# A decoder layer on one core: reordering the background work of cross-attention, and the maxima rows' way into the operand stack

## The reference

```python
# _L0_xattn_ref(target, source, ...): 16 heads of 16, 512 positions t (targets) and s (sources)
q = Wq @ layernorm(x)  + bq        # [256, 512]
k = Wk @ ctx + bk
v = Wv @ ctx + bv
# per head: scores = q^T k / sqrt(16), masked; softmax over s; out = probabilities @ v
# x2 = x + out, then the feed-forward
```

## Time and profile before

| | us |
|---|---|
| median of 3 runs | 2346.96 (2342.14 to 2351.12) |
| profiled execution | 2347.5, its span 2345.7 |
| TensorE busy | 2167.7 (92%) |
| VectorE busy | 1597.0 (68%) |
| ScalarE, GpSimd busy | 797.7, 761.3 |
| main loop of the cross-attention | 1500.2 to 2047.3 of the span |

### The profile page before, as it was taken

How to read it: one execution, slowest core, us unless ns; L and a number is a source line. 1 busy time by engine, 2 the same in 40 slices (tenths; PEclk the granted TensorE clock), 3 DMA queues, 4 the chain that set the end, 5 groups by cost and what they waited for, 6 DMA issues and landing times. The chain is left out here.

```text
span 2345.7 us, 35412 instructions
## 1 busy us (share of the span) xinstructions
PE 2167.7 (92%) x11638; PEld 1524.1 (65%) x11638; DVE 1597.0 (68%) x2871; ACT 797.7 (34%) x1845; POOL 761.3 (32%) x533
## 2 busy tenths in 40 slices
PE   6899999999999999999999997599888899879998
PEld 4677777778787777778778785233333333267776
DVE  6658888788786558788788774477777778542221
ACT  1323323322323323323323322155555546642221
POOL 3235334434444334434434433211122221212121
PEclk9999999999999999999999998798989978989999
DMA  5211011011102201011101006634555434311110
GB/s 197 87 40 52 16 49 51 24 40 51 46 19 99 82 20 52 24 41 51 43 22 51 32 4 118 114 64 81 93 107 90 87 74 84 99 60 54 54 36 19
DMA packets 58981, 142.27 MB, mean 61 GB/s; under 512 B 9118, under 2 KB 23910, under 8 KB 53894
## 3 DMA queue, kind: packets, MB, share of 16 engines
q1 hardware_dynamic: 57142, 138.98, 23.4%
q10 hardware_dynamic: 1744, 2.08, 0.3%
HBM read 89.93 MB, written 17.55 MB: 46 GB/s over the span
## 5 line engine op out<-in xcount | busy, mean ns | idle before, releaser
L1614 DVE TENSOR_REDUCE x_mx<-x_pm 128x1 f32<-128x512 f32 x512 | 316.5, 680 | 58.2 <-PE x_pm L1706 55.8
L1472 ACT ACTIVATE x_E<-x_pd 128x512 f32<-128x512 f32 x512 | 264.8, 604 | 214.1 <-PE x_pd L1720 213.4
L1083 PE MATMUL a_pj<-q_big,a_wqk_h 128*128 128x512 f32 x1024 | 290.1, 405 | 1.4 <-POOL a_wqk_l L628 1.4
L1099 PE MATMUL a_pj<-a_wvg_h,q_big 128*128 128x512 f32 x1024 | 286.0, 406 | 1.1 <-DVE a_rm L787 1.0
L1099 PEld LDWEIGHTS a_pj<-a_wvg_h,q_big 128*128 128x128 f32 x1024 | 185.4, 188 | 51.8 <-DVE a_rm L787 2.4
L787 DVE TENSOR_TENSOR a_rm<-a_pj,a_rope 128x1024 f32<-128x1024 f32 x128 | 155.7, 1218 | 79.9 <-PE a_pj L1083 78.5
L1083 PEld LDWEIGHTS a_pj<-q_big,a_wqk_h 128*128 128x128 f32 x1024 | 182.9, 188 | 40.8 <-POOL a_wqk_l L628 1.9
L520 ACT ACTIVATE a_v<-a_pj 128x256 f32<-128x256 f32 x128 | 49.1, 384 | 415.6 <-PE a_pj L1099 415.6
L660 POOL TENSOR_TENSOR a_ogl<-a_ogf,a_ogh 128x512 fp32r<-128x512 f32 x64 | 81.7, 1298 | 285.4 <-ACT a_ogf L556 285.4
L1734 PE MATMUL x_pa<-x_E,x_vx 128*32 128x512 f32 x1024 | 152.2, 670 | 0.0
L859 DVE TENSOR_TENSOR a_acc<-a_po,a_acc 128x512 f32<-128x512 f32 x128 | 85.9, 687 | 92.7 <-PE a_po L1212 92.7
(11 more groups left out here) (219 smaller groups left out, 4624.9 us busy)
## 6 DMA issues: line engine op xcount, KB each, us to landing
a_qk_raw<-in_wqk SPq DMA_DIRECT2D x16, 1024.0 KB, 5.5
a_vg_raw<-in_wvg SPq DMA_DIRECT2D x16, 1024.0 KB, 4.9
a_wo_raw<-in_wo SPq DMA_DIRECT2D x16, 512.0 KB, 3.7
x_Q<-x_hi SPq DMA_DIRECT2D x20, 256.0 KB
x_K<-x_hi SPq DMA_DIRECT2D x20, 256.0 KB
a_acc<-in_w SPq DMA_DIRECT2D x6, 704.0 KB, 4.4
a_wt<-in_w SPq DMA_DIRECT2D x24, 176.0 KB, 2.3
weights_scratch<-a_wt SPq DMA_DIRECT2D x24, 176.0 KB, 1.9
```

The costliest lines, as they stand in the source:

```text
L1083: last = mm(pj[:, j % 2, :], wa[:, c, j * P:(j + 1) * P], xa[:, c, p * UT:(p + 1) * UT], start=k == 0, stop=k == 11)
L1099: last = mm(pj[:, tt % 2, :], xa[:, c, t0:t0 + P], wa[:, c, :], start=k == 0, stop=k == 11)
L1472: nc.scalar.activation(E[:, n % ESLOTS, :], pd[:, n % 3, :], ACT.Exp, scale=XD ** -0.5).then_inc(exp_done, 1)
L1614: nc.vector.reduce_max(mx[:, u % 2, at:at + 1], pm[:, k % 3, :], AX_X).then_inc(pm_done, 1)
```

## The change

- Projections of batch b + 2 move from G5 to G10 to G7 to G12, in the order key, query, value; takes, high halves and low halves with them (ScalarE's high halves to G8 to G11).
- The row statistics go to G5 and G6, both norms to G8, the inversions of the sums to G7 to G12 (in the last two batches one a step from G2 and from G10).
- On GpSimd the second `divide_and_add` goes between the key and the query low halves.
- SyncE: new FILLS and LATE; the load of x at G2 and not at G13 of the batch before; the stores at G3 and G15.
- The maxima rows go from mT straight to Q. VectorE's `max_rows` now waits for the landing of the previous quad's row.
- wv, the identity and the bf16 identity are loaded once, in stage one, and stay in SBUF. TensorE waits for the cross-attention's other constants two value projections later.
- At the end of stage one the low halves of the last output are subtracted by VectorE from PSUM; ogf isn't written there.

```diff
+        def order(b):
+            return (2, 3, 0, 1, 4, 5) if b > 1 else (0, 1, 2, 3, 4, 5)
         def projected(b, j):
-            return 6 * b + j - 4
+            return 6 * b + order(b).index(j) - 4
+        def halved(b, w):
+            return 4 * (b - 1) + order(b).index(2 * w + 1) + 1
+        def inverses(b, G):
+            if b + 2 < B:
+                due = {7: (-1, (0, 1)), 8: (-1, (2,)), 9: (-1, (3,)), 10: (0, (0,)), 11: (0, (1, 2)), 12: (0, (3,))}
+            else:
+                due = {**{2 + i: (-1, (i,)) for i in range(4)}, **{10 + i: (0, (i,)) for i in range(4)}}
+            n, parts = due.get(G, (0, ()))
+            return 2 * b + n, (parts if 2 * b + n >= 0 else ())
...
-        FILLS = {8: ((0, 0),), 10: ((0, 1), (0, 2)), 11: ((0, 3), (0, 4)), 14: ((0, 5), (1, 0)), 15: ((1, 1), (1, 4))}
-        LATE = {0: ((1, 5),), 2: ((1, 2), (1, 3))}
+        FILLS = {10: ((1, 0), (1, 1)), 11: ((1, 4), (1, 5)), 12: ((0, 0), (0, 1)), 13: ((0, 2),), 14: ((0, 3), (1, 2)), 15: ((1, 3), (0, 4))}
+        LATE = {0: ((0, 5),)}
...
             def rows(u):
                 sp.wait_ge(pm_done, turned_slot(u) + 1)
                 after(sp, row_in[u % 2], 32 * (u // 2))
-                sp.dma_start(max_dram[u % 2], mT[:].bitcast(F32)).then_inc(max_out, 16)
-                sp.wait_ge(max_out, 16 * u + 16)
                 for e in range(2):
                     sp.dma_start(Q[b % 3][64 * e + 53:64 * e + 54, 2 * g:2 * g + 2].rearrange("p h t -> p (h t)").bitcast(F32),
-                                 max_dram[u % 2, 8 * e:8 * e + 8, :].rearrange("(o a) t -> o (a t)", o=1)).then_inc(row_in[u % 2], 16)
+                                 mT[8 * e:8 * e + 8].bitcast(F32)).then_inc(row_in[u % 2], 16)
...
-                    if q == 3 and t >= 4 and t % 2 == 0:
-                        store(t // 2 - 2)
+                    if b and G in (3, 15):
+                        store(2 * b - 2 + (G == 15))
                     if b + 2 < B:
+                        if G == 2 and b:
+                            load_x(b + 2)
...
-                        if G == 13 and b + 3 < B:
-                            load_x(b + 3)
...
             def max_rows(u):
-                after(dve, max_out, 16 * u)
+                if u:
+                    dve.wait_ge(row_in[(u - 1) % 2], 32 * ((u - 1) // 2 + 1))
...
-                    if q >= 2 and t >= 2 and t % 2 == 0:
-                        invert(t // 2 - 1, q - 2)
-                    if q < 2 and t >= 3 and t % 2 == 1:
-                        invert((t - 3) // 2, q + 2)
                     G = 4 * (t % 4) + q
+                    n, parts = inverses(b, G)
+                    for i in parts:
+                        invert(n, i)
                     if b + 2 < B:
-                        if G < 2:
-                            norm_stats(b + 2, G)
-                        if 3 <= G < 5:
-                            norm(b + 2, G - 3)
-                        if 5 <= G < 11:
-                            take_projection(b + 2, G - 5)
+                        if 5 <= G < 7:
+                            norm_stats(b + 2, G - 5)
+                        if G == 8:
+                            norm(b + 2, 0)
+                            norm(b + 2, 1)
+                        if 7 <= G < 13:
+                            take_projection(b + 2, order(2)[G - 7])
...
             quad_scores(0, 1)
-            pe.wait_ge(const_in, N_CONST)
             project(0, 4)
             quad_scores(0, 2)
             project(0, 5)
             quad_scores(0, 3)
+            pe.wait_ge(const_in, N_CONST)
             project(1, 0)
...
+            def low_last(l):
+                for h in range(2):
+                    dve.wait_ge(ogh_done, 2 * l + h + 1)
+                    nc.vector.tensor_tensor(ogl[:, h, :], po[:, h, :], ogh[:, h, :].bitcast(F32), ALU.subtract).then_inc(ogl_done, 1)
```

More of the change, by code:

```diff
@@ L554, in high_out @@
                     nc.scalar.activation(ogh[:, h, :], po[:, h, :], ACT.Copy).then_inc(ogh_done, 1)
-                    after(act, ogl_done, 2 * l)
-                    nc.scalar.activation(ogf[:, h, :], po[:, h, :], ACT.Copy).then_inc(ogf_done, 1)
+                    if not final(l):
+                        after(act, ogl_done, 2 * l)
+                        nc.scalar.activation(ogf[:, h, :], po[:, h, :], ACT.Copy).then_inc(ogf_done, 1)
             def unit(n, g, p, k0):
@@ L1003, in core @@
                 gated(m, pm)
+                low_last(m)
                 normalised(5)
@@ L1492, in _ @@
                     G = 4 * (t % 4) + q
-                    if 6 <= G < 10 and t // 4 + 2 < B:
-                        high(t // 4 + 2, G - 6)
+                    if 8 <= G < 12 and t // 4 + 2 < B:
+                        high(t // 4 + 2, order(2)[G - 8])
             take_weighted(QUADS - 1)
@@ L1552, in _ @@
                     rsqrt(b + 2)
-                    for j in range(4):
-                        low(b + 2, j)
+                    low(b + 2, 2)
+                    low(b + 2, 3)
+                if b:
+                    divide_and_add(2 * b - 1)
+                if b + 2 < B:
+                    low(b + 2, 0)
+                    low(b + 2, 1)
                     values(b + 2, 0)
                     values(b + 2, 1)
-                if b:
-                    divide_and_add(2 * b - 1)
             divide_and_add(2 * B - 2)
@@ L1597, in take_projection @@
                         dve.wait_ge(x_in[1], 32)
-                    elif j == 0:
+                    elif b > 1 and j == order(b)[0]:
                         dve.wait_ge(stack_in[(b - 1) % 3], stacked(b - 1))
@@ L1766, in _ @@
                     G = 4 * (t % 4) + q
-                    if 5 <= G < 11 and b + 2 < B:
-                        project(b + 2, G - 5)
+                    if 7 <= G < 13 and b + 2 < B:
+                        project(b + 2, order(2)[G - 7])
                     if t + q:
@@ L1771, in _, with feed_forward @@
             weighted(QUADS - 1, 3)
-def feed_forward(nc, signals, spent, x2_in, raw, big, ident_in, identb_in, out):
+def feed_forward(nc, signals, spent, x2_in, raw, big, ident, identb, out):
     G = N_TOK // 512
@@ L2112, in decoder @@
                        x1.rearrange("(h b) t p d -> h p (b t) d", h=HALVES), a["w"], scalers, rebuilt, weights,
-                       big, xs, a["ctx"], a["mask"], a["wq"], a["wk"], a["bqk"], rows)
+                       big, xs, ident, identb, wv_t, a["ctx"], a["mask"], a["wq"], a["wk"], a["wv"], a["bqk"], a["identb"], rows)
         with Scope(nc, "x") as passing:
@@ L2117, in decoder @@
         w_raw = kept.sb("raw", [P, 3, NFLAT], BF16)
-        cross_attention(nc, of_cross, of_self.used, x1, a["ctx"], a["mask"], a["maskc"], a["wq"], a["wk"], a["wv"], a["bqk"], a["bv"],
-                        a["ident"], rows, maxima, x2, third, bv_t, w_raw, weights, big, xs)
+        cross_attention(nc, of_cross, of_self.used, x1, a["ctx"], a["mask"], a["maskc"], a["wq"], a["wk"], wv_t, a["bqk"], a["bv"],
+                        ident, rows, x2, third, bv_t, w_raw, weights, big, xs)
         of_self.close()
         of_ffn = kept.enter_context(Scope(nc, "sf"))
-        feed_forward(nc, of_ffn, of_cross.used, x2.rearrange("(g b) t p d -> g (b t) p d", b=2), w_raw, big, a["ident"], a["identb"],
+        feed_forward(nc, of_ffn, of_cross.used, x2.rearrange("(g b) t p d -> g (b t) p d", b=2), w_raw, big, ident, identb,
                      out.rearrange("(g b) (t p) d -> g (b t) p d", b=2, p=P))
```

49 lines of the change are left out of this document (21 added, 28 removed).

## The result

| | us |
|---|---|
| changed kernel | 2329.4 median of 20 runs (2306.14 to 2350.48) |
| kernel before, same chips | 2352.26 median of 20 runs (2342.14 to 2371.45) |
| ratio | 0.9876, 95% interval 0.9852 to 0.9899 |
| profiled execution | 2321.17, span 2319.4 (before 2345.7) |

What follows compares the result with a forecast made beforehand. It took VectorE's waits for late loads and sums, which stop TensorE and lower its clock in the cross-attention, as the bound. Terms -51.9, -6.0, -5.8, -3.0, -1.4, -1.6 sum to -69.7: 2277 us, range 2264 to 2290, or 2303 with the next rival's better half.

Steps and rivals of the forecast that it cites:

- Projections, inversions and statistics moved: Batches 1 to 5 of the cross-attention: with every DMA wait gone they take 307.5 us for 359.40, -51.9 us.
- Every one has cover: Batches 1 to 5: each load and sum arrives before its reader needs it, the thinnest being x at G5, 2 us or so.
- Maxima rows sent straight into the stack: Main loop, 32 rows: one DMA and one SyncE wait fewer per quad, 2.04 us hidden in quiet quads; nothing extra gained.
- price of the undisturbed batch: One of batches 1 to 5 where nothing is late: four quads of 12.40 us plus six projections, 61.5 us.
- working by quads: Batches 1 to 5 priced from undisturbed quads at 12.40 us and projections at 1.85 or 2.13 us each: -51.9 us.
- rival in which it is slower: The direct row, written in small pieces into one partition, takes longer than both hops: 2360 us or more, chance 0.02.
- Batch 0: Without statistics in G0, quad 1 starts after 25.4 us for 35.26, less 4.1 us clock recovery: -5.8 us.
- Batch 6: Its first quad, 18.40 us at clock 0.63, falls to 12.40 with a direct row and fills spread out: -6.0 us.
- Constants and the end of stage one: Two loads less ahead of the main loop, -3.0 us; last low halves on VectorE straight from PSUM, -1.4 us.
- Feed-forward and all behind: Feed-forward start: both identities stay in SBUF, so TensorE doesn't wait for a load, -1.6 us.
- the loads are as late as before, only elsewhere: Rival: a wait at G5 or G7 costs 10.5 us a batch; 2329 for all five batches; chance 0.12.
- The clock falls all the same: Rival: in batches 1 to 5 small gaps still lower TensorE's clock, 2297 at one fall per batch, to 2318; chance 0.18.

Runs made afterwards that it cites:

- row-first kernel: The changed kernel with the next quad's maxima row issued in a quad's first step, ahead of `spread`, not in the second behind it: 2301.06 us, ratio 0.977.
- runs with a wait on purpose: The fastest kernel with TensorE's first dot product in seven quads also waiting for two or five unused GpSimd operations: 2301.25 us (0.9773) and 2352.64 us (1.0006).
- fastest kernel: The row-first kernel with batch 0's first row ahead of key pieces and x loads, and the last two batches' first inversions at G5 to G8: 2269.48 us, ratio 0.9653.
- direct row alone: The kernel before, with the maxima rows sent straight from mT into the stack and nothing else of the change: 2329.37 us, ratio 0.9893.
- run with the statistics in G0 and G1: The row-first kernel with row statistics back in G0 and G1, the x load at G13, the second store at G11: 2306.94 us, ratio 0.9814.

## Why the prediction was wrong, point by point

**The step that failed** is in "Projections, inversions and statistics moved": "Every one has cover", with its twin in "Maxima rows sent straight into the stack", "the row is issued in the second step of four, at least two steps or 6.2 us before the next quad". The count went by places in SyncE's list and by bytes in a step. It checked the loads and the sums against the bulk, and not the row at G13, which it took at the quiet hop's 2.04 us, though its own has a hop behind pieces that was back only after 10.4 us. The row's way is longer: SyncE comes to it 3.4 us after its step begins, since the wait and the issue of `spread` and the issue of two pieces of G12 stand ahead in the list, and then its transfer stands behind those pieces. It got 5.5 us for the 6.2 and needed 6.8; what was mis-sized most is the landing, 6.8 for 2.04, and 6.2 us of cover would have been too short as well. The term was -51.9; it measured 345.05 - 359.40 = -14.4. By place in the batch, against the undisturbed 12.20, 14.76, 20.38, 14.13, the five batches lost 22.5 us in their first quads, 8.5 in their second, nothing in their third and 6.7 in their last.

**What held in it** is the price of the undisturbed batch: 61.5 us forecast, 61.47 in the row-first kernel, whose five batches took 308.55, -50.9 for the -51.9. The quad with both norms and four projections took 20.38, within the 12.40 + 4 x 2.13 = 20.9 of the forecast's prices, so VectorE's G8 costs nothing that shows, as taken. The Trainium skill (TensorE: Matmul & The Clock Gate, Terms) led to 65.1 us for the same batches, of which 39.5 are its price of the low clock and 25.6 VectorE's waits, added by the prediction. The 50.9 measured once the batches are undisturbed decide: the working by quads was right, this estimate 14 us too much. The runs with a wait on purpose say that the price of the clock has a share in it: with granted clocks of 0.984, 0.969 and 0.946 over the spans that price would be 35 and 91 us more than in the fastest kernel, and 22.8 and 61.3 were measured beyond the waits.

**The direct row** was taken at nothing, "counted above" where it was late; both ways round it measured some 25 us, and the new order without it gives nothing one can measure. The rival in which it is slower was not borne out.

**Batch 0**: forecast -5.8, measured 78.85 against 84.4 (1500.20 to 1584.60), -5.5; its first quad was 26.29 for 25.4, stopped by the maxima row for 14.13 us as said, and the clock was 0.81 in the second. The recovery there cost 16.71 - 14.76 = 1.9 us for the 4.1 forecast, and the late row at the batch's end took 1.3 us that the forecast had not counted: that the sum comes out so close is partly luck. **Batch 6**: forecast -6.0 for the first quad, measured 17.45 for 18.40, -1.0, again by a row late behind fills. Even the 1.0 is no gain of the quad. The window of the earlier trace rows begins 0.9 us before the first dot product, in the row's wait:

```profile
1944.94 0.49 PE L1720 MATMUL x_pd<-q_big 54*128 54x512 f32 x2 [1.19 <-DMA q_big<-maxima_scratch]
```

Cut there the quad is 17.4 us before and after, and the five batches before are 360.35, so that 15.3 of the forecast 51.9 came and nothing of the 6.0. The direct row alone did give 12.78 there; with the new order it is late again. **Constants and the end of stage one**: forecast -4.4, measured 1496.25 for 1500.20, -4.0. TensorE's wait at the end of stage one is 1.50 for 2.97 us, the -1.4 forecast; from there to the main loop it took 44.7 for 49.4 us, -4.7 for the -3.0 and within its bound of -5 (the clock rises sooner, the second value projection took 1.99 us for 3.65); and stage one itself came 2.2 us later, which nothing explains. **Feed-forward and all behind**: before, 2345.7 - 1962.4 = 383.3 us remained after that quad; now 2319.4 - 1937.60 = 381.8; -1.5 for the forecast -1.6. The five lines add up to the 26 us between the spans: one large term was mis-sized by 37.5 us and one small one by 5 (36.6 and 6.0 with the cut at the dot product).

**The rivals.** What came is nearest to "the loads are as late as before, only elsewhere" (2329 for all five, 2329.4 measured), but at another place than named: at G5 and G7 nothing waits, the late transfer is the maxima row at each border. That the two numbers agree is chance: the rival charged five batches 52.5 us, where 37.5 were missing, and made its sum for the profiled execution, which took 2321.17. It had 0.12 and should have had far more. "The clock falls all the same" isn't what happened in the changed kernel: with the same small gaps every quad of batches 1 to 5 has 1.00 once the row is early. But it isn't refuted in general: in the run with the statistics in G0 and G1 the clock fell in three of five first quads without a wait of TensorE over 0.72 us. The Trainium skill (the same page, A second HAM failure mode) tells of falls from short idles between groups of matmuls as the PSUM banks are cycled; in the row-first kernel the gaps of 0.2 to 0.4 us in every step, and one of 0.8 us in each batch, didn't bring one, waits of 0.7 and of 1.1 us elsewhere sometimes did.

**Open:** why the same wait of 1.3 us lowers the clock at one border and hardly at the next, and why it comes back within a quad here and after 30 us there. That may be why the changed kernel's runs spread over 44 us and the fastest one's over 8, but no run shows it. Open is also how the gain of the statistics' move divides from that of the load's.

## What to carry to other kernels

Cover of a small urgent DMA is counted from the time its issuing engine can reach it: go through what stands ahead of it in the list, waits included, and put it first, with the bulk behind. Moving bulk about without moving the urgent one only moves the place where it is late. Price a wait of TensorE not at its length but, where it comes at the border of quads in a stage like this one, at some four times that (3.8 and 3.7 here), and look for the wait in the quad before the one with the low clock.

## What the runs showed that was not expected

- A wait of TensorE of 1.14 us was enough for its clock to fall to 1.2 GHz in four cases of seven, one of 3.2 us in seven of seven; one of 0.77 us was enough once in the fastest kernel (its second quad of batch 4, 16.20 us at 0.89).
- Once low it stayed low though TensorE's row shows no idle time. In the changed kernel, over 30 us of batch 3:

```profile
1711.00:1741.00 30.00, 30.00 (x107) 10.69 (x103) 17.09 (x32) 14.42 (x28) 0.71 (x1) 0.51 0.53 111
```

- The two DMAs of a direct row keep SyncE's queue for 1.43 us, where the second hop's two took 0.53; it is still the better way.
